# Delta-rule stage of a four-block kernel: GpSimd's additions wait for the second batch's transitions, two products change PSUM banks, and TensorE begins four tiles of output earlier

## The reference, cut to what matters

```python
# b = 2 sequences, h = 4 heads, n = 32 chunks of 32 tokens, dk = dv = 32
A = einsum('bhncd,bhned->bhnce', k*beta, k)
T = inv(eye + tril(A, -1))            # per chunk
u = T @ (v*beta);  w = T @ (k*beta)
def body(S, inp):                     # a scan over the 32 chunks
    q_i, k_i, u_i, w_i = inp
    attn = where(tri, q_i @ k_i.T, 0.0)
    u_i = u_i - w_i @ S
    o_i = q_i @ S + attn @ u_i
    S = S + k_i.T @ u_i
    return S, o_i
local_mix = p0*v + p1*short_filter(v) + p2*long_filter(v)
o = w_global*o + (1 - w_global)*local_mix     # then norm over dv, and @ Wo
```

## Time and profile before

| | |
|---|---|
| time, median of 3 runs | 624.46 us (624.46, 609.24, 624.79) |
| profiled execution, its own time | 602.81 us |
| its span in the trace | 601.1 us |
| mean granted TensorE clock | 0.986 of full |
| PE busy | 546.1 us (91%) |
| DVE busy | 407.1 us (68%) |
| ACT busy | 324.2 us (54%) |
| POOL busy | 174.4 us (29%) |

### The profile page before, as it was taken

How to read it: one execution, slowest core, us unless ns; L and a number is a source line. 1 busy time by engine, 2 the same in 40 slices (tenths; PEclk the granted TensorE clock), 3 DMA queues, 4 the chain that set the end, 5 groups by cost and what they waited for, 6 DMA issues and landing times.

```text
span 601.1 us, 17481 instructions
## 1 busy us (share of the span) xinstructions
PE 546.1 (91%) x7472; PEld 373.3 (62%) x7472; DVE 407.1 (68%) x773; ACT 324.2 (54%) x574; POOL 174.4 (29%) x333
## 2 busy tenths in 40 slices
PE   4799999999999999999999996996999779897993
PEld 2445555555555557777777785774667667565672
DVE  5697999999999826263545337345899871576774
ACT  2327888788888876655555645556422330125441
POOL 7000111445535422010101006246982560010101
PEclk9899999999999999999999999898999999999998
DMA  4778667374240000001000000021673300000011
GB/s 118 153 224 212 190 149 147 81 154 79 57 104 7 5 2 2 0 7 31 1 2 1 0 1 0 2 36 39 124 93 73 73 4 4 5 1 1 1 36 35
DMA packets 54051, 33.82 MB, mean 56 GB/s; under 512 B 38853, under 2 KB 45509, under 8 KB 53974
## 3 DMA queue, kind: packets, MB, share of 16 engines
q1 hardware_dynamic: 48822, 31.65, 23.8%
q10 hardware_dynamic: 5152, 1.05, 1.1%
HBM read 20.83 MB, written 9.44 MB: 50 GB/s over the span
## 4 chain that ended last, share of the span: by engine, by line
PE 70%; DVE 13%; ACT 6%; DMA 6%; issue 2%; SPq 1%; POOL 1%; POOLq 0%; ACTq 0%; DVEq 0%
PE ps L1760 10%; PE ps L1745 9%; PE ps L1512 7%; PE ps L1514 6%; PE ps L1513 6%; PE ps L1860 6%; DMA qst<-shift_sb 4%; PE ps L1724 3%; PE ps L1933 2%; PE ps L2065 2%; DVE filtered L1344 2%; PE ps L2066 2%; ACT prob L682 2%; PE ps L1926 2%; PE ps L1602 1%
## 5 line engine op out<-in xcount | busy, mean ns | idle before, releaser
L1203 DVE TENSOR_REDUCE nmx<-ps 128x1 f32<-128x1024 f32 x128 | 154.1, 1218 | 16.6 <-PE ps L1725 15.2
L682 ACT ACTIVATE prob<-ps 128x512 f32<-128x512 f32 x256 | 137.4, 597 | 26.6 <-PE ps L1745 26.1
L1760 PE MATMUL ps<-prob,vp 128*32 128x128 f32 x2048 | 78.9, 278 | 0.0
L1745 PE MATMUL ps<-qst,kst 50*128 50x512 f32 x256 | 73.6, 492 | 4.7 <-ACT prob L682 3.5
L1760 PEld LDWEIGHTS ps<-prob,vp 128*32 128x32 f32 x2048 | 49.2, 109 | 39.8 <-ACT prob L682 22.4
L1076 DVE TENSOR_TENSOR h_lo<-hf,h_hi 128x512 fp32r<-128x512 f32 x48 | 33.1, 690 | 52.4 <-ACT h_hi L591 50.2
L1512 PE MATMUL ps<-h_hi,w_lo 128*128 128x512 f32 x144 | 58.1, 403 | 2.4 <-DVE h_lo L1076 2.4
L1514 PE MATMUL ps<-h_hi,w_hi 128*128 128x512 f32 x144 | 57.0, 396 | 0.0
L1513 PE MATMUL ps<-h_lo,w_hi 128*128 128x512 f32 x144 | 56.9, 395 | 0.0
L1724 PE MATMUL ps<-kst,qst 48*128 48x512 f32 x128 | 52.6, 412 | 2.2 <-DMA kst<-k_scratch 1.6
L1725 PE MATMUL ps<-kst,qst 48*128 48x512 f32 x128 | 51.5, 404 | 0.0
(11 more groups left out here) (248 smaller groups left out, 1102.3 us busy)
## 6 DMA issues: line engine op xcount, KB each, us to landing
qst<-q_scratch SPq DMA_DIRECT2D x31, 192.0 KB, 4.5
kst<-k_scratch SPq DMA_DIRECT2D x31, 192.0 KB, 4.8
w_raw<-L_ffn_h_w SPq DMA_DIRECT2D x8, 256.0 KB, 3.9
kd<-ka SPq DMA_DIRECT2D x8, 256.0 KB, 6.5
X<-L_attn_x SPq DMA_DIRECT2D x4, 256.0 KB, 5.0
qst<-shift_sb SPq DMA_DIRECT2D x64, 4.0 KB
q_scratch<-w_hi SPq DMA_DIRECT2D x2, 512.0 KB, 5.0
k_scratch<-w_lo SPq DMA_DIRECT2D x2, 512.0 KB, 3.3
```

Of the source, the lines that this page charges most:

```text
L682: nc.scalar.activation(prob[:, n % PROBS, GT * (t % 2):GT * (t % 2) + GT], ps[:, RINGB + i % RING, :], ACT.Exp, scale=SCORE_SCALE).then_in ...
L1203: nc.vector.tensor_reduce(nmx[:, u % 2, j:j + 1], pair, AX.X, ALU.max, negate=True).then_inc(max_done, 1)
L1745: nc.tensor.matmul(ps[:, RINGB + i % RING, :], kst[r:r + 50, p, P * t:P * t + P], half_of(qst[r:r + 50, p, :], u % 2), start=True, stop=Tr ...
L1760: last = nc.tensor.matmul(ps[32 * j:32 * j + 32, PVB, P * half:P * half + P], vp[:, h, t, :], prob[:, n % PROBS, c:c + P], start=(t == 0), ...
```

## The change

1. `MG_BANK` is (0, 0) and `B_BANK` is (6, 6). The order of banks inside the transition products is turned round (half of the tiles first, then pair), so VectorE reads them through a view with one more dimension, with the same elements for each instruction. Tiles 0 to 3 of the transition products now wait for two copies of u and w, tiles 4 to 7 for all four.
2. GpSimd's wait for `uw_psum` 2, the zeroing of the first state and the wait for `g_ready` 2 stand ahead of all eight additions, not ahead of the last four.
3. TensorE: `begin_outputs(0, 0..3)` stands between `inputs_of_state(0)` and `times_inverse(1)`. The waits for `m_ready` 2 and `g_ready` 2 ahead of its old place are gone there; the same two waits still stand once, ahead of the scan.
4. keep_busy: 5 and 3 products in bank 5 around `inputs_of_state(0)` (5 and 8 in bank 7 before); 6 in bank 7 ahead of `inputs_of_state(1)` and none behind it (5 and 2 in bank 3 before).

```diff
--- before.py
+++ after.py
@@ -251,7 +251,7 @@
     sw2 = wc_flat[:, FB * FH:FB * FH + FB * D].rearrange("p (k n) -> p k n", k=FB)
     xt_hi, xt_lo = x_lo_flat[:, GT:2 * GT], x_lo_flat[:, 2 * GT:3 * GT]
 
-    FIR_BANK, UW_BANK, MG_BANK, B_BANK = (0, 4), (4, 0), (0, 4), (4, 0)
+    FIR_BANK, UW_BANK, MG_BANK, B_BANK = (0, 4), (4, 0), (0, 0), (6, 6)
     OT_BANK, Y4_BANK, X3T_BANK = 2, 3, (2, 1, 1, 1)
 
     with nc.Block() as block:
@@ -1018,11 +1018,10 @@
                                                vtok[:, 4 * g:4 * g + 4, :].rearrange("p n (h e) -> p n h e", h=4),
                                                per_head(mixw[:, 4 * g:4 * g + 4, 0:12:3]), ALU.mult)
             link(last)
+            pool.wait_ge(uw_psum, B)
+            nc.gpsimd.memset(state[:, 0], 0.0).then_inc(state_zeroed, 1)
+            pool.wait_ge(g_ready, 2)
             for i, g in enumerate(FINAL):
-                if i == 2:
-                    pool.wait_ge(uw_psum, B)
-                    nc.gpsimd.memset(state[:, 0], 0.0).then_inc(state_zeroed, 1)
-                    pool.wait_ge(g_ready, 2)
                 v4 = vtok[:, 4 * g:4 * g + 4, :].rearrange("p n (h e) -> p n h e", e=C)
                 pool.wait_ge(weighted, i + 1)
                 link(nc.gpsimd.tensor_tensor(v4, v4, filtered_tok[:, 0, g], ALU.add))
@@ -1322,16 +1321,17 @@
                 dve.wait_ge(mg_psum, b + 1)
 
                 def product(c, a):
-                    pair = ps[:, MG_BANK[b] + 2 * (c // 2):MG_BANK[b] + 2 * (c // 2) + 2, :].rearrange("p k (n x) -> p (k n) x", x=4 * C)
+                    both = ps[:, MG_BANK[b]:MG_BANK[b] + 4, :].rearrange("p (k q) (n x) -> p k q n x", q=2, x=4 * C)
                     o = 2 * C * a + C * (c % 2)
-                    return pair[:, :, o:o + C]
+                    return both[:, :, c // 2, :, o:o + C]
 
                 for c in range(4):
-                    last = nc.vector.tensor_tensor(mt[:, b, c], eye32[:].rearrange("p (o e) -> p o e", o=1).broadcast_to([P, 8, C]),
+                    last = nc.vector.tensor_tensor(mt[:, b, c].rearrange("p (k n) e -> p k n e", k=2),
+                                                   eye32[:].rearrange("p (k o e) -> p k o e", k=1, o=1).broadcast_to([P, 2, 4, C]),
                                                    product(c, 0), ALU.subtract)
                 last.then_inc(m_ready, 1)
                 for c in range(4):
-                    q = qs[:, S * b:S * b + S].rearrange("p (n c t) -> p c n t", n=8, c=4)[:, c]
+                    q = qs[:, S * b:S * b + S].rearrange("p (k n c t) -> p c k n t", k=2, n=4, c=4)[:, c]
                     last = nc.vector.tensor_tensor(q, q, product(c, 1), ALU.subtract)
                 last.then_inc(g_ready, 1)
 
@@ -1906,11 +1906,11 @@
             def transition_products(b):
                 pe.wait_ge(kd_in[b], 4 * 16)
                 for n in range(8):
-                    pe.wait_ge(uw_ready, 4 * b + n // 2 + 1)
+                    pe.wait_ge(uw_ready, 4 * b + 2 * (n // 4) + 2)
                     for p in range(2):
                         r = pair(p)
                         for h in range(4):
-                            last = nc.tensor.matmul(ps[32 * h:32 * h + 32, MG_BANK[b] + 2 * p + n // 4, 4 * C * (n % 4):4 * C * (n % 4) + 4 * C],
+                            last = nc.tensor.matmul(ps[32 * h:32 * h + 32, MG_BANK[b] + 2 * (n // 4) + p, 4 * C * (n % 4):4 * C * (n % 4) + 4 * C],
                                                     uw(b, r, n, h)[:, 32:64], kd[b][r, n, h].rearrange("p a d e -> p (a d e)"), start=True, stop=True)
                 last.then_inc(mg_psum, 1)
 
@@ -1938,21 +1938,18 @@
             times_inverse(0)
             pe.wait_ge(fir_tok_ready, 8)
             transition_products(0)
-            keep_busy(7, 5)
+            keep_busy(5, 5)
             inputs_of_state(0)
-            keep_busy(7, 8)
+            keep_busy(5, 3)
             pe.wait_ge(m_ready, 1)
             pe.wait_ge(g_ready, 1)
+            for n in range(4):
+                begin_outputs(0, n)
             times_inverse(1)
             pe.wait_ge(b_ready, 1)
             transition_products(1)
-            keep_busy(3, 5)
+            keep_busy(7, 6)
             inputs_of_state(1)
-            keep_busy(3, 2)
-            pe.wait_ge(m_ready, 2)
-            pe.wait_ge(g_ready, 2)
-            for n in range(4):
-                begin_outputs(0, n)
             pe.wait_ge(state_zeroed, 1)
 
             def o_region(b, n, c, h):
```

## The result

The changed kernel takes 620.29 us (median of 4 runs, 619.82 to 622.2). Timed beside it, the kernel before had 624.46, 609.24, 624.79 and 605.62 us, a median of 616.85. The ratio is 1.027, with a 95% interval of 1.022 to 1.031: **slower by 2.7%**. That ratio leaves the two runs of the kernel before near 624 us out; with them in, the two medians are only 3.4 us apart. What those two runs very likely had is what the change brought into all four of its runs: a lower granted clock. By hand, 620.29 over 605.62 is 1.024, and over the 602 us that the same kernel mostly takes in the experiments 1.030, so the loss is 2 to 3%.

The account below looks back on a forecast made before the run. VectorE's chain of waits up to the scan was taken as the bound; the terms put step 1 at 491.55 against 492.24 us, so 624.46 - 0.7 = 623.8 us, range 606 to 627.

Parts of the forecast that it names:

- what bounds the kernel now: Opening step: VectorE's unbroken chain from 468.56 to 490.12 us; the change's worth is how much earlier than 492.24 step 1 starts.
- Rival C: Clock falls in the 3.1 us pause at the stop at 473.3 us: net +1.6 us, 626.1 us; chance 0.12.
- the sum: Path from times_inverse(1) to step 1 at 491.55 against 492.24 us: 0.7 us gained, carried to the median as 623.8 us.
- `weigh`: VectorE's eight multiplications: four stay at 1.45 us beside GpSimd, the last four fall to 0.68 each.
- Code stop: About 12 instructions into begin_outputs, TensorE waits for a late code page, from 473.3 to 476.45 us.
- Copies, transition products, state inputs: Batch 1, behind times_inverse(1): ScalarE's copies 2.05 us, inputs_of_state(1) 1.72; next code pages given 0, bound 0.3.
- Step 1: First step of the scan: starts at 491.55 us against 492.24, 0.7 us earlier.
- GpSimd's start beside the copy: Ahead of the scan, the first state's copy, due at 490.4 us, stands behind GpSimd's second addition, until 491.4.
- the variant that the sum named: The first state's copy slips between two GpSimd additions: 1.5 us gained instead of 0.7.
- keep_busy: 24 products become 18, at 0.265 us each; the six ahead of inputs_of_state(1) cost 1.6 us on the new path.
- Rival B: Code in time, no stop at 473.3 us: step 1 starts 3.4 to 4.4 us earlier, 620.1 to 621.1 us; chance 0.25.
- D: Gain given back in the later stream through shifted code pages or unmoved work: 0 to -0.3 us, 624.3 us; chance 0.13.

Follow-up runs that it names:

- the burst: The changed kernel with 16 more products that nobody reads in step 6 of the scan (17, not 1): 607.71 us (10 runs), ratio 1.008.

## Why the prediction was wrong

**The step that failed** is in "what bounds the kernel now": "nothing in the diff changes a step", and the change being worth "one number", the start of step 1. The diff changed no step's instructions, but it took away what stood in front of them. Before, `begin_outputs` ran right up to step 1, without a pause. It was TensorE's cover for the copies of the inputs and of the first state; moved away, it left a pause. The pause stands in my own sum: state inputs to 489.1, step 1 at 491.55, 2.4 us (measured 2.67). I summed it as waiting time and asked nothing more of it. Rival C priced a fall of the clock only at the other pause, with 5.8 us of work behind it. Its mechanism was the right one, its place and therefore its price were not: there a short fall came as well (3.4 us from 478.6), and cost `times_inverse(1)` 1.5 us (5.49 against 3.95); in front of the scan it cost 16.1. Nor did its bounds hold, "a pause between 1.96 us (no fall today) and 4.1 (a fall)": a fall followed a pause of 1.61 us, and none followed one of 3.22. Why the clock, once down, stayed down through the scan is not shown; that it did, and that filling the pause prevents it, is.

The second failure is in "the sum": "what makes that I can't read from one trace, and I carry the difference over to the median". The clocks of the two runs at 624 us are not on record; in the later runs of the same kernel one mean clock for each run separates the groups (0.932 at 622.72 us against 0.984 at 601.74), so the two were most likely runs with a long fall of the clock. The forecast of 623.8 us is near the measured 620.29 by luck: it took over a base from runs of the kernel before whose clock had most likely fallen, and the changed kernel's clock fell for another reason, the pause. From the two other executions then known, 602.81 and 609.24 us, the same sum gives 602.1 to 608.5 us.

Point by point, the rest:

- *`weigh`*: four at 1.45 and four at 0.68 us was the forecast, 8.5 us; measured 8.38. `sw0` took 0.68 us, the lower bound.
- *Code stop*: predicted 12 instructions into `begin_outputs`; it came behind 6 loads and 6 MATMULs, at 475.39 us, for 1.47 us. Right in place, and half as long as forecast: on this trace's time my sum had TensorE stop at 474.3 and go on at 477.4, it stopped 1.1 us later and went on 0.5 us earlier (476.87).
- *Copies, transition products, state inputs*: 2.06, 2.05 and 1.69 us against 2.05, 2.03 and 1.72. No stop for code inside them, as forecast. Batch 0 had a small one that the sum didn't have, 0.44 us inside `inputs_of_state(0)`.
- *Step 1*: forecast 29.1 us behind the start of `times_inverse(0)`, measured 29.85. The 0.8 us are less than the 1.5 us of the short fall. So the 0.7 us of gain that the whole forecast was about didn't come: step 1 was 0.1 us later.
- *GpSimd's start beside the copy*: forecast as standing behind the second addition; it was, 1.25 us; in the profiles with two products in each step and with the burst the same copy took 0.20 us, which is the variant that the sum named. The end of the additions was covered. The 1.45 us of GpSimd's multiplications were set against the 1.26 of its additions, another operation; no run has the multiplications alone.
- *keep_busy*: priced as path time only (0.265 us each), with no word of what the two behind `inputs_of_state(1)` and the work around them did for the clock.
- *Rival B* didn't come, since the stop did. For *D* the two profiles have no more than 0.4 us behind the last step.

## What to carry to other kernels

Before work is moved away from in front of a chain of small matmuls, write down which intervals of TensorE become empty, and ask of each at which clock the stage behind it will run: step 1 came only 0.1 us later here, with a pause of 2.67 us in front of it, and the stage behind it took 16 us longer, because the clock didn't come back until the scan was over. Where no real work fits, a few products into a bank that is free by then (here behind one wait for `g_ready`) were worth more than they cost, directly in front of the chain. Whether they must stand there, in one piece, wasn't tested; inside the scan 17 in one piece lifted the clock, and one more in each step didn't. Where the times of one kernel come in two groups, compare the mean granted clock of the runs before anything else, and put the forecast on the group with the same clock.

## What the runs showed that I hadn't expected

The scan is a stage with two ways to run. By their mean clocks 17 of 86 runs of the kernel before had a long fall, nine a shorter one. In six profiles the clock fell ahead of the scan or in its first 3 us. In five of them it came back only 51 to 55 us later: in four kernels (the changed one, the ones with GpSimd's part put back, with the added pause, with three products) behind the scan's last step, in the one with two products in each step about 3 us ahead of it. Only 17 products in one piece brought it back early. It isn't a matter of small products alone: in the attention block of one profile, with large ones, the clock stayed at half for 34 us too. What ends such a fall is open. A fall can also come in the midst of the scan without a pause of more than some tenths of a us.

A second: stops of 0.2 to 3.2 us among small TensorE instructions, with nothing to wait for, at a place that, in the one case tried, moved by as many instructions as were put ahead of it; I read them as code that comes late. The Trainium skill describes the pages (Runtime: NRT & Kernel Launch, Instruction fetch mechanics) and takes their cost as mostly hidden; in these traces it is not, in stretches where a page lasts about 2 us.
